# Five steps of the last slab moved from the seventh turn into the last one

## The chip, the cores and the metric

The kernel runs on one core of a Trainium2 chip. A core has a matrix engine (TensorE, PE in the profile; PEld are its weight loads), VectorE (DVE), ScalarE (ACT), GpSimd (POOL) and SyncE (SP), which here only issues DMAs. Each engine works through its own queue in order, and the queues wait for each other by semaphores. The metric is the device time of one execution in microseconds (us).

## The reference

2048 tokens (4 sequences of 512) are looked up in a table of 256 channels. An RWKV-7 attention layer follows (4 heads of 64 channels, a recurrence over the 512 positions), then a mixture of 8 experts, of which each token takes the likeliest.

```python
h = take(table, x) + bias
# attention on u = layernorm(h); xr, xw, xk, xv, xa, xg are mixes of u with its predecessor
r, k, v = xr @ Wr, xk @ Wk, xv @ Wv
a = sigmoid(a0 + xa @ a1 @ a2);  g = sigmoid(xg @ g1) @ g2
# ... kk, the decay w, and k changed by a; then for each position
S = S * wd + (S @ (-kk)) (kk * a)^T + v k^T;  y = S @ r
y = groupnorm(y) * ln_w + ln_b
y = y + (r * k * r_k).sum(per head) * v          # the bonus
h = h + (y * g) @ Wo
# experts
n = layernorm(h);  logits = (n @ w_red) @ normed(wg).T
e = argmax(softmax(logits));  score = max(softmax(logits))
h = h + score * (gelu(n @ W1[e] + b1[e]) @ W2[e] + b2[e])
```

## The kernel before

**Tiling.** The 512 positions are cut into 16 tiles of 32 positions by 4 sequences, 128 rows each, and two tiles make a slab; there are SLABS = 8 slabs. One call `build` emits the whole program, and every engine has a function `emit(step, i)` that holds what this engine does in a named step of slab i. All engines walk one list of (step, slab), made by `turns()` from two lists that are written out by hand: ORDER, with a step and by how many slabs it runs ahead of the turn (`P.lg:1` is done in turn 6 for slab 7), and LAST, the order of the last turn and of the expert tiles. Nothing is planned at run time.

**Steps.** F and P steps make a slab's inputs to the recurrence. P.lv (line 1019) makes the low-rank projection of v, and in the same PSUM bank the logits' share of the slab's own rows and, for a slab three back (BEHIND), the share of its attention output zT. P.lg (1063) is g's first product and ScalarE's sigmoid (460), after which ScalarE goes back to its table with ln and exp. P.rt (1082) sums r*k*r_k per head, ScalarE copies the sums to el_T (482). R.e (1030) turns el_T to token order; VectorE reads from it rt, emb_lg and the logits of the slab three back (751). P.kP, P.ar, P.bP scale keys and queries by the decay, P.tokk and P.tokb (1087, 1093) turn them to token order, P.M makes the products within a slab, P.masks masks them. P.g (1068) is g's second product; ScalarE copies the gate (464), GpSimd multiplies it with ln_w to gw (329). P.q is GpSimd's alone: v times rt, plus ln_b, times the gate, qg (336). Q steps are the recurrence of a slab: X0, T0 to X3, T3 an inverse by halves, W, A, S the state and the output y for its two tiles. O steps are the group norm of y, gw and qg, the turn to zT (O.zT), the product with Wo (O.out) and the addition to the rows (O.add). Z.l (1040) makes logits from zT directly, for slabs from ALONE on; Z.c takes the largest. N steps are the second norm.

**What sets the order around the change.** PSUM banks are shared by name: bank 0 by P.lv, R.e, P.lg, P.tokk and P.g, bank 1 by P.rt and P.tokb, bank 7 by O.zT, Z.l, O.out and the state. P.tokk waits for el_kept and rt_ok, by which VectorE has read R.e (1089). Q.A0's second half waits for logits_ok when a slab lies behind ALONE (1203). In the last turn G and H steps count and list the rows of each expert (G for slabs 0 to 6, H for slab 7), SP writes the rows and then the norm's scalars to `kept` (275), GpSimd fetches rows by the lists from there (T.f, line 379) and writes results (T.s, 371). SP waits for qg_ok before the first scalars, GpSimd before the first fetch, and VectorE before G.list. The T steps are the 23 expert tiles: T.n norms, T.x turns (1378), T.h is the first product (1391) and gelu, T.o the second (1404).

The list that repeats in every turn, unchanged by the diff:

```python
ORDER = """Q.X0:0 F.xn:2 P.norm:1 O.red:-1 Q.T0:0 E.norm:2 P.v:1 Q.X1:0 P.lv:1 Q.T1:0 P.lwa:1 F.xT:2 E.turn:2 O.yn:-1 N.st:-2
Q.X2:0 P.vga:1 F.xx:2 Q.T2:0 E.fold:2 P.key:1 P.wup:1 Q.W0:0 O.zT:-1 P.lg:1 N.rs:-2 Q.X3:0 P.cum:1 P.vc:1 N.lm:-2 P.decay:1
P.rt:1 Q.T3:0 R.e:1 Z.l:-1 Q.A0:0 P.kP:1 P.ar:1 P.tokk:1 P.bP:1 Q.S0:0 P.k:2 P.M:1 F.stats:3 F.rstd:3 E.out:1 P.q:1 O.out:-1
Q.W1:0 P.g:1 Z.c:-2 O.add:-1 Q.A1:0 P.tokb:1 P.masks:1 Q.S1:0 O.sq:0 P.r:2""".split()
```

Of the kernel before, what the change touches and what calls it, by code (L numbers as in the profile page):

```python
# [19 lines left out]
NT = BLK * L  # L20
# [11 lines left out]
ALONE = SLABS - BEHIND  # L32
# [53 lines left out]
def build(nc, table, tokens, tok_bias, consts, W, w1, w2, a1, a2, v1, v2, g1, g2, wo_t, w_red, wg, W1, W2, b2, kept, out):  # L86
    ctx = ExitStack()
    with ctx:
# [213 lines left out]
        def _(pool):  # L302
# [11 lines left out]
            def emit(step, i):  # L314
# [75 lines left out]
        def _(act):  # L390
# [12 lines left out]
            def emit(step, i):  # L403
# [33 lines left out]
                elif step == "P.lv":  # L437
# [3 lines left out]
                    rows = slice(64, 64 + L + E if i >= BEHIND else 64 + E)  # L441
# [18 lines left out]
                elif step == "P.lg":  # L460
                    act.wait_ge(s["lg_ps"], n)
# [1022 lines left out]
```

## Time and profile before

| | us |
|---|---|
| median of 3 runs | 482.14 |
| the runs | 479.24, 482.14, 486.59 |
| the profiled execution | 479.76 |
| its span in the profile | 477.6 |

The span runs from the first to the last instruction; 2.2 us lie around it. In the profile a line L1046 is line 1046 of the kernel, and a step is known by its line. PEclk is the TensorE clock that was granted, as a share of 2.4 GHz: 0.50 is 1.2 GHz. An fp32 product counts as two matmuls. Matmuls overlap, so the us of neighbouring rows add up to more than the time between their starts.

### The profile page before, as it was taken

The page shows a single profiled execution, that of the slowest core. Times are in us where ns is not written, and L with a number is a line of the kernel's source. Part 1 is how long each engine was busy: PE and PEld are TensorE (multiplying, and loading weights), DVE is VectorE, ACT ScalarE, POOL GpSimd, SP SyncE. Part 2 cuts the span into 40 slices and gives each one's busy share as a digit, 9 for nine tenths or more (in the row PEclk, how much of TensorE's full clock was granted, in tenths as well). Part 3 has the DMA queues.
Part 4 walks back from the last instruction along what each step waited for, and adds up shares of the span by engine and source line. Part 5 has one row for each costly group of instructions (what it writes and reads, how often), then busy time and mean ns, then how long its engine had stood idle before and what let it go on. Part 6 is the DMA issues. An engine that isn't in the chain of part 4 may idle for free.

```text
span 477.6 us, 23442 instructions
## 1 busy us (share of the span) xinstructions
PE 419.4 (88%) x10651; PEld 337.1 (71%) x10651; DVE 307.3 (64%) x784; ACT 200.2 (42%) x418; POOL 168.6 (35%) x153
## 2 busy tenths in 40 slices
PE   0467999999999998999999999897896898999991
PEld 0345777777867876877777776786785797889981
DVE  3646878578478678859768857736387654545541
ACT  1276484484385376367347526411111341222220
POOL 4754422342433425215315313403002336545231
PEclk9996899999999999999999999876586899999996
DMA  8960000000000000000000000000004557656310
GB/s 275 323 268 1 3 5 4 4 4 5 27 4 5 27 3 5 25 5 4 4 27 4 5 26 5 3 26 5 4 16 137 219 190 254 208 188 195 111 44 23
DMA packets 14014, 32.15 MB, mean 67 GB/s; under 512 B 4121, under 2 KB 7068, under 8 KB 13788
## 3 DMA queue, kind: packets, MB, share of 16 engines
q1 hardware_dynamic: 10908, 22.47, 14.1%
q0 software_dynamic: 3008, 8.19, 5.2%
q8 instruction: 84, 1.38, 1.2%
q14 instruction: 14, 0.11, 0.1%
HBM read 25.50 MB, written 5.15 MB: 64 GB/s over the span
## 4 chain that ended last, share of the span: by engine, by line
PE 63%; issue 11%; DVE 7%; POOL 6%; ACT 6%; DMA 5%; POOLq 0%; DVEq 0%; ACTq 0%; SPq 0%
PE ps L970 7%; PE ps L977 6%; POOL out L371 4%; PE ps L982 4%; PE ps L1107 3%; PE ps L1391 3%; DMA arena<-kept,arena 2%; PE ps L989 2%; POOL arena L379 2%; PE ps L1249 2%; PE ps L1175 2%; PE ps L1058 2%; PE ps L1404 2%; PE ps L1081 2%; PE ps L1066 1%
## 5 line engine op out<-in xcount | busy, mean ns | idle before, releaser
L595 DVE SCALAR_TENSOR_TENSOR arena<-arena 128x256 f32<-128x256 f32 x96 | 47.8, 546 | 5.1 <-PE ps L1028 2.9
L1404 PE MATMUL ps<-arena 128*128 x184 | 44.4, 383 | 2.3 <-issue 1.3
L1391 PE MATMUL ps<-arena 128*128 128x128 f32 x368 | 46.3, 281 | 0.0
L1391 PEld LDWEIGHTS ps<-arena 128*128 128x128 f32 x368 | 45.6, 198 | 0.8
L371 POOL DMA_INDIRECT out<-arena x23 | 22.7, 985 | 51.2 <-DVE arena L929 50.6
L551 ACT ACTIVATE arena<-arena 128x512 f32<-128x512 f32 x23 | 14.5, 629 | 61.6 <-DVE arena L917 61.6
L1404 PEld LDWEIGHTS ps<-arena 128*128 128x128 f32 x184 | 33.1, 190 | 7.8 <-issue 4.0
L379 POOL DMA_INDIRECT arena<-kept,arena x23 | 22.5, 979 | 43.0 <-DMA kept<-arena 35.5
L970 PE MATMUL ps<-arena 128*128 128x256 f32 x128 | 35.5, 427 | 0.7 <-DVE arena L595 0.7
L977 PE MATMUL ps<-arena 128*128 128x256 f32 x128 | 34.7, 417 | 0.0
L322 POOL TENSOR_TENSOR arena<-arena 128x512 f32<-128x512 f32 x8 | 8.4, 1046 | 64.7 <-ACT arena L436 64.7
L970 PEld LDWEIGHTS ps<-arena 128*128 128x128 f32 x128 | 26.0, 213 | 5.7 <-issue 0.8
L977 PEld LDWEIGHTS ps<-arena 128*128 128x128 f32 x128 | 25.0, 205 | 4.7 <-issue 0.6
L925 DVE TENSOR_TENSOR arena<-ps,arena 128x256 f32<-128x256 f32 x23 | 9.8, 424 | 27.2 <-PE ps L1404 26.1
L343 POOL TENSOR_TENSOR arena<-arena 128x512 f32<-128x512 f32 x8 | 10.1, 1268 | 47.9 <-ACT arena L466 47.9
L396 ACT ACT_TABLE_LOAD x20 | 25.7, 1283 | 1.0 <-PEq L1476 0.8
L917 DVE TENSOR_TENSOR arena<-ps,arena 128x512 f32<-128x512 f32 x23 | 15.9, 690 | 13.2 <-PE ps L1391 13.1
L1000 PE MATMUL ps<-arena 128*128 128x128 f32 x32 | 5.6, 303 | 19.9 <-ACT arena L413 16.9
L319 POOL TENSOR_TENSOR arena<-arena 128x512 f32<-128x512 f32 x8 | 10.2, 1275 | 32.5 <-DVE arena L606 32.4
L982 PE MATMUL ps<-arena 65*128 65x256 f32 (+1 forms) x64 | 18.9, 420 | 1.0 <-issue 1.0
L1000 PEld LDWEIGHTS ps<-arena 128*128 128x128 f32 x32 | 3.6, 150 | 22.6 <-issue 22.6
L307 POOL DMA_INDIRECT arena<-table,arena x16 | 16.3, 1020 | 9.0 <-DMA arena<-tokens 4.4
(315 smaller groups left out, 1046.3 us busy)
## 6 DMA issues: line engine op xcount, KB each, us to landing
arena<-W SPq DMA_DIRECT2D x23, 514.0 KB, 5.0
arena<-W SPq DMA_DIRECT2D x8, 512.0 KB, 8.3
kept<-arena SPq DMA_DIRECT2D x8, 256.0 KB, 2.4
arena<-W SPq DMA_DIRECT2D x4, 256.0 KB, 4.8
arena<-b SPq DMA_DIRECT2D x1, 1024.0 KB, 15.9
arena<-consts SPq DMA_DIRECT2D x1, 849.0 KB, 4.8
arena<-kept,arena POOLq DMA_INDIRECT x23, 4.8
out<-arena POOLq DMA_INDIRECT x23, 2.5
```

Of the source, the lines that this page charges most:

```text
L307: pool.indirect_dma_start(out=res[:, t, :], out_offset=None, in_=table[:, :], in_offset=bass.IndirectOffsetOnAxis(ap=ids[:, t:t + 1], axis ...
L371: pool.indirect_dma_start(out=out[:, :], out_offset=bass.IndirectOffsetOnAxis(ap=(rows_u if i < FIRST else out_u)[:, i:i + 1], axis=0), in ...
L379: pool.indirect_dma_start(out=x_s[q % XB], out_offset=None, in_=kept[0:1 + 128 * (T1 if q < FIRST else TILES), :], in_offset=bass.Indirect ...
L396: A.preload_act_table_set(name)
L551: A.activation(hT[i % 2], h_pre[i % 2], ACT.Gelu).then_inc(s["act_ok"], 1)
L595: last = V.scalar_tensor_tensor(out=mix[j % 3][:, p, :], in0=xx[:, p].rearrange("p b t -> p (b t)"), scalar=mixed_by[MIXES[j]][:, p:p + 1] ...
L917: V.tensor_tensor(h_pre[b], ps[:, 2 + b, :].rearrange("p (m t) -> p m t", m=HC), W1_s[i % WB][:, 2 * HID:2 * HID + HC].unsqueeze(2).broadc ...
L970: last = mul(pair(ps[:, bank, :], h2), w[:, kt, h2 * 128:(h2 + 1) * 128], src[:, kt, :], start=kt == 0, stop=kt == 1)
L977: last = mul(ps[:, bank, c * C:(c + 1) * C], src[:, kt, c * 128:(c + 1) * 128], w[:, kt, :], start=kt == 0, stop=kt == 1)
L982: last = mul(ps[:, bank, c * C:(c + 1) * C], src[0:rows, c * 128:(c + 1) * 128], w[0:rows, :], start=True, stop=True)
L1391: last = mul(ps[:, 2 + b, m * 128:(m + 1) * 128], W1_s[i % WB][:, p * HID + m * 128:p * HID + (m + 1) * 128], x_sT[b][:, p, :], start=p == ...
L1404: last = mul(ps[:, 1, b * C:(b + 1) * C], hT[b][:, m, :], W2_sb[:, bass.ds(e * (HC * C) + m * C, C)], start=m == 0, stop=m == HC - 1)
```

## The change

ALONE goes from 5 to 4, so that slab 4's logits are made by a Z.l step of their own in turn 5, and P.lv and R.e of the last slab no longer carry them. P.rt, R.e, P.lg, P.g and P.q of slab 7 (HELD) leave turn 6 and stand in LAST, where Q.X0:7, Q.T0:7, Q.X1:7, Q.T1:7 and later steps are around them. LAST is a new list also beyond that: N.st:5 and N.rs:5, G and H steps and the expert tiles stand in another order. The waits follow: for slab 7, P.rt waits until bank 1 was read (tokb_ok), R.e until bank 0 was (tokk_ok), P.lg until VectorE has read R.e, P.g until the sigmoid is done; P.tokk waits for lv_ok in place of R.e's readers. In the last turn ScalarE loads the sigmoid's table before P.lg and the one of ln and exp behind it. The diff, cut to its changed lines, the lists to their beginnings:

```diff
 BEHIND = 3
-ALONE = SLABS - BEHIND
+ALONE = SLABS - BEHIND - 1
 T2 = TILES - T1
...
-LAST = """Q.X0:7 O.red:6 Q.T0:7 O.yn:6 Q.X1:7 Z.c:5 Q.T1:7 O.zT:6 Q.X2:7 N.st:5 N.rs:5 Z.l:6 Z.c:6 Q.T2:7 Q.W0:7 N.lm:5 Q.X3:7 G.cnt:0 Q.T3:7 Q.A0:7
-G.rank:0 Q.S0:7 Q.W1:7 Q.A1:7 Q.S1:7 O.out:6 O.sq:7 G.list:0 O.add:6 N.st:6 N.rs:6 O.red:7 N.lm:6 G.dif:0 G.exp:0 O.yn:7 G.score:0 G.own:0
-G.turn:0 O.zT:7 Z.l:7 G.rows:0 T.f:0 Z.c:7 H.cnt:0 H.rank:0 O.out:7 T.n:0 T.x:0 H.list:0 T.n:1 T.x:1 H.own:0 T.h:0 T.n:2 T.n:3 T.h:1 T.x:2
-O.add:7 N.st:7 T.o:0 N.rs:7 N.lm:7 H.dif:0 T.s:0 T.n:4 H.exp:0 H.score:0 T.x:3 T.n:5 T.h:2 T.o:1 T.x:4 T.s:1 H.turn:0 T.h:3 T.o:2 T.h:4 T.s:2
-H.rows:0 T.n:6 T.f:1 T.x:5 T.o:3 T.n:7 T.x:6 T.h:5 T.o:4 T.n:8 T.x:7 T.h:6 T.x:8 T.n:9 T.s:3 T.o:5 T.h:7 T.n:10 T.s:4 T.o:6 T.x:9 T.n:11 T.s:5
...
+LAST = """Q.X0:7 P.rt:7 O.red:6 Q.T0:7 R.e:7 O.yn:6 Q.X1:7 Z.c:5 P.lg:7 Q.T1:7 N.st:5 P.g:7 O.zT:6 Q.X2:7 Z.l:6 Z.c:6 Q.T2:7 N.rs:5 Q.W0:7 Q.X3:7 N.lm:5
+G.cnt:0 Q.T3:7 Q.A0:7 G.rank:0 Q.S0:7 Q.W1:7 Q.A1:7 Q.S1:7 O.out:6 G.list:0 O.add:6 O.sq:7 N.st:6 N.rs:6 O.red:7 N.lm:6 G.dif:0 G.exp:0 P.q:7
+O.yn:7 G.score:0 O.zT:7 G.own:0 G.turn:0 Z.l:7 G.rows:0 Z.c:7 H.cnt:0 H.rank:0 O.out:7 T.f:0 T.n:0 T.x:0 H.list:0 T.n:1 T.x:1 T.n:2 T.n:3
+T.h:0 T.x:2 H.own:0 T.h:1 T.o:0 T.n:4 T.x:3 T.n:5 T.h:2 O.add:7 T.s:0 T.o:1 T.s:1 T.x:4 N.st:7 N.rs:7 H.turn:0 T.n:6 N.lm:7 H.dif:0 H.exp:0
+H.score:0 T.h:3 T.x:5 T.o:2 T.s:2 H.rows:0 T.h:4 T.o:3 T.x:6 T.h:5 T.f:1 T.o:4 T.n:7 T.h:6 T.x:7 T.n:8 T.n:9 T.s:3 T.o:5 T.x:8 T.s:4 T.h:7
+T.x:9 T.s:5 T.o:6 T.n:10 T.s:6 T.n:11 T.h:8 T.x:10 T.n:12 T.o:7 T.h:9 T.x:11 T.o:8 T.h:10 T.x:12 T.s:7 T.n:13 T.n:14 T.o:9 T.h:11 T.s:8 T.s:9
...
+HELD = ["P.rt", "R.e", "P.lg", "P.g", "P.q"]
...
         for step, ahead in steps:
-            if 0 <= turn + ahead < SLABS:
+            if 0 <= turn + ahead < SLABS - (step in HELD):
                 yield step, turn + ahead
...
                 elif step == "P.g":
+                    if i == SLABS - 1:
+                        pool.wait_ge(s["g_ok"], n)
                     last = P.tensor_tensor(gw[par], gate, ln_w.unsqueeze(1).broadcast_to([128, CH, C]), ALU.mult)
...
                     after(act, "el_ps", i)
-                    rows = slice(64, 64 + L + E if i >= BEHIND else 64 + E)
+                    rows = slice(64, 64 + L + E if BEHIND <= i < SLABS - 1 else 64 + E)
                     A.copy(el_T[rows, :], ps[rows, 0, 0:NT]).then_inc(s["lv_ok"], 1)
...
                 elif step == "P.lg":
+                    if i == SLABS - 1:
+                        use("sigmoid_and_others")
                     act.wait_ge(s["lg_ps"], n)
-                    A.activation(low_g, ps[:, 0, 0:NT], ACT.Sigmoid)
+                    last = A.activation(low_g, ps[:, 0, 0:NT], ACT.Sigmoid)
+                    if i == SLABS - 1:
+                        last.then_inc(s["la_ok"], 1)
                     use("natural_log_exp_and_others")
...
                                     sd1[:, tiles].unsqueeze(2).broadcast_to([128, CH, E]), ALU.mult).then_inc(s["el_kept"], 1)
-                    if i >= BEHIND:
+                    if BEHIND <= i < SLABS - 1:
                         past = slice((i - BEHIND) * CH, (i - BEHIND + 1) * CH)
...
                     pe.wait_ge(s["fold_ok"], 2)
-                    if i >= BEHIND:
+                    if BEHIND <= i < SLABS - 1:
                         pe.wait_ge(s["fold_ok"], 3)
                         last = mul(ps[64:64 + L, 0, 0:NT], wl[:, kt, :], xT[:, kt, 1:CH + 1, :].rearrange("p c t -> p (c t)"), start=kt == 0, stop=kt == 1)
-                        if i >= BEHIND:
+                        if BEHIND <= i < SLABS - 1:
                             last = mul(ps[96:96 + E, 0, 0:NT], wol[:, kt, :], zT[:, kt, :], start=kt == 0, stop=kt == 1)
                     pe.wait_ge(s["invp_ok"], n)
+                    if i == SLABS - 1:
+                        pe.wait_ge(s["tokk_ok"], n)
                     after(pe, "el_kept", i)
                     for c in range(CH):
-                        m = 96 + E if i >= BEHIND else 64 + E
+                        m = 96 + E if BEHIND <= i < SLABS - 1 else 64 + E
                         last = nc.tensor.transpose(ps[:, 0, c * 128:c * 128 + m], el_T[0:m, c * 128:(c + 1) * 128], ident[0:m, 0:m])
...
                     after(pe, "xT_ok", i + 2, 1 * SLABS)
+                    if i == SLABS - 1:
+                        pe.wait_ge(s["el_kept"], n)
+                        pe.wait_ge(s["rt_ok"], n)
                     for kt in range(2):
                     pe.wait_ge(s["tokk_ok"], n)
+                    if i == SLABS - 1:
+                        pe.wait_ge(s["la_ok"], n + 1)
                     up_by_token(g2_sb, low_g, 0, 128).then_inc(s["g_ps"], 1)
...
                     pe.wait_ge(s["rk_ok"], n)
+                    if i == SLABS - 1:
+                        pe.wait_ge(s["tokb_ok"], n)
                     for h2 in range(2):
                     pe.wait_ge(s["kP_ok"], n)
-                    pe.wait_ge(s["el_kept"], n)
-                    pe.wait_ge(s["rt_ok"], n)
-                    after(pe, "logits_ok", i - BEHIND + 1)
+                    if i < SLABS - 1:
+                        pe.wait_ge(s["el_kept"], n)
+                        pe.wait_ge(s["rt_ok"], n)
+                        after(pe, "logits_ok", i - BEHIND + 1)
+                    else:
+                        pe.wait_ge(s["lv_ok"], n)
                     to_tokens(kP, 0).then_inc(s["tokk_ps"], 1)
```

## Rows read from the trace of the kernel before

**Rows 1.** Windows by turn: stretch, its length, each engine's busy us, PEclk, DMA, GB/s

```profile
246.60:284.40 37.80, 37.23 (x1261) 28.34 (x1264) 28.39 (x67) 21.15 (x43) 12.64 (x10) 1.00 0.04 12
284.40:324.00 39.60, 37.48 (x1251) 29.12 (x1254) 23.53 (x55) 16.60 (x34) 12.18 (x10) 0.87 0.03 10
324.00:372.90 48.90, 37.62 (x1050) 32.29 (x1038) 31.14 (x128) 6.33 (x18) 7.29 (x7) 0.65 0.20 62
```

**Rows 2.** Timeline of turn 5, TensorE: start, us, line, out<-in, count

```profile
266.35 0.67 PE L1200 MATMUL ps<-arena 32*32 32x64 f32 x32
...
269.76 1.99 PE L970 MATMUL ps<-arena 128*128 128x256 f32 x8
...
275.93 1.11 PE L1249 MATMUL ps<-arena 32*32 32x64 f32 x64
```

**Rows 3.** Timeline of turn 6, TensorE; in brackets idle before and its releaser

```profile
299.25 1.03 PE L1066 MATMUL ps<-arena 128*128 128x256 f32 x4
...
302.39 0.63 PE L1085 MATMUL ps<-arena 128*32 128x256 f32 x4
302.95 0.75 PE L1167 MATMUL ps<-arena 32*32 32x32 f32 x64
303.99 0.37 PE L1038 MATMUL ps<-arena 104*128 104x104 f32 x2 [0.28 <-ACT arena L485]
304.87 1.03 PE L1046 MATMUL ps<-arena 128*128 128x8 f32 x8 [0.51 <-DVE arena L761]
305.83 0.66 PE L1200 MATMUL ps<-arena 32*32 32x64 f32 x32
...
317.56 1.11 PE L1249 MATMUL ps<-arena 32*32 32x64 f32 x64
...
319.71 1.13 PE L982 MATMUL ps<-arena 128*128 128x256 f32 x4
```

**Rows 4.** Windows of turn 6 and the last turn, columns as in the first

```profile
307.00:316.00 9.00, 8.58 (x220) 7.20 (x217) 3.89 (x15) 0.58 (x1) 0.00 (x0) 0.50 0.01 4
...
324.00:327.00 3.00, 1.67 (x140) 1.33 (x128) 2.15 (x4) 1.11 (x3) 0.00 (x0) 1.00 0.02 5
327.00:331.00 4.00, 2.25 (x128) 1.98 (x128) 3.26 (x11) 0.00 (x0) 2.35 (x2) 0.50 0.03 6
331.00:345.00 14.00, 12.29 (x415) 10.94 (x419) 5.65 (x25) 1.46 (x4) 0.17 (x1) 0.50 0.02 5
```

**Rows 5.** Timeline, VectorE and ScalarE, in turn 6 and the last turn

```profile
300.70 1.28 ACT L396 ACT_TABLE_LOAD   x1
301.02 0.41 DVE L705 TENSOR_TENSOR arena<-ps,arena 128x256 f32<-128x256 f32 x1
302.00 0.30 ACT L517 ACTIVATE arena<-arena 128x2 f32<-128x2 f32 x1
...
332.38 0.58 ACT L554 COPY arena<-ps 128x512 f32<-128x512 f32 x1 [5.62 <-PE ps L1323]
```

**Rows 6.** Timeline of the last turn, TensorE

```profile
325.65 0.74 PE L1124 MATMUL ps<-arena 32*32 32x32 f32 x63 [0.93 <-DVE arena L678]
...
327.97 1.08 PE L1131 MATMUL ps<-arena 32*32 32x32 f32 x64 [1.00 <-DVE arena L684]
...
331.23 1.11 PE L1323 MATMUL ps<-arena 128*128 128x128 f32 x4 [0.47 <-POOL arena L350]
332.28 1.08 PE L1145 MATMUL ps<-arena 32*32 32x32 f32 x64
...
344.66 1.08 PE L1200 MATMUL ps<-arena 32*32 32x64 f32 x32 [0.52 <-DVE arena L709]
```

**Rows 7.** Timeline of the last turn, VectorE

```profile
349.25 0.34 DVE L951 TENSOR_SCALAR arena<-arena 128x128 f32<-128x128 f32 x1
...
356.12 0.69 DVE L736 TENSOR_TENSOR arena<-ps,arena 128x512 f32<-128x512 f32 x1 [0.45 <-PE ps L977]
```

**Rows 8.** Timeline of the expert tiles, TensorE

```profile
399.35 0.44 PE L1378 MATMUL ps<-arena 128*128 128x128 f32 x2 [1.82 <-DVE arena L913]
```

More of the change, by code:

```diff
@@ L57 @@
-O.add:7 N.st:7 T.o:0 N.rs:7 N.lm:7 H.dif:0 T.s:0 T.n:4 H.exp:0 H.score:0 T.x:3 T.n:5 T.h:2 T.o:1 T.x:4 T.s:1 H.turn:0 T.h:3 T.o:2 T.h:4 T.s:2
-H.rows:0 T.n:6 T.f:1 T.x:5 T.o:3 T.n:7 T.x:6 T.h:5 T.o:4 T.n:8 T.x:7 T.h:6 T.x:8 T.n:9 T.s:3 T.o:5 T.h:7 T.n:10 T.s:4 T.o:6 T.x:9 T.n:11 T.s:5
-T.h:8 T.x:10 T.o:7 T.h:9 T.x:11 T.s:6 T.o:8 T.n:12 T.s:7 T.h:10 T.x:12 T.o:9 T.n:13 T.h:11 T.x:13 T.s:8 T.o:10 T.s:9 T.s:10 T.n:14 T.n:15
-T.h:12 T.x:14 T.n:16 T.o:11 T.h:13 T.o:12 T.x:15 T.h:14 T.s:11 T.s:12 T.n:17 T.x:16 T.n:18 T.o:13 T.h:15 T.x:17 T.n:19 T.o:14 T.s:13 T.h:16
@@ L61 @@
-T.x:18 T.n:20 T.o:15 T.h:17 T.x:19 T.s:14 T.o:16 T.h:18 T.n:21 T.s:15 T.x:20 T.n:22 T.o:17 T.h:19 T.s:16 T.x:21 T.o:18 T.h:20 T.s:18 T.x:22
-T.s:17 T.o:19 T.s:19 T.h:21 T.o:20 T.s:20 T.h:22 T.o:21 T.s:21 T.o:22 T.s:22""".split()
+LAST = """Q.X0:7 P.rt:7 O.red:6 Q.T0:7 R.e:7 O.yn:6 Q.X1:7 Z.c:5 P.lg:7 Q.T1:7 N.st:5 P.g:7 O.zT:6 Q.X2:7 Z.l:6 Z.c:6 Q.T2:7 N.rs:5 Q.W0:7 Q.X3:7 N.lm:5
+G.cnt:0 Q.T3:7 Q.A0:7 G.rank:0 Q.S0:7 Q.W1:7 Q.A1:7 Q.S1:7 O.out:6 G.list:0 O.add:6 O.sq:7 N.st:6 N.rs:6 O.red:7 N.lm:6 G.dif:0 G.exp:0 P.q:7
@@ L63 @@
+T.x:13 T.o:10 T.s:10 T.h:12 T.x:14 T.o:11 T.n:15 T.h:13 T.x:15 T.n:16 T.n:17 T.s:11 T.o:12 T.h:14 T.x:16 T.o:13 T.h:15 T.s:12 T.o:14 T.s:13
+T.x:17 T.h:16 T.n:18 T.o:15 T.x:18 T.s:14 T.n:19 T.s:15 T.h:17 T.n:20 T.x:19 T.n:21 T.o:16 T.h:18 T.x:20 T.n:22 T.o:17 T.h:19 T.x:21 T.s:16
+T.o:18 T.s:18 T.h:20 T.x:22 T.s:17 T.o:19 T.h:21 T.s:19 T.o:20 T.h:22 T.s:20 T.o:21 T.s:21 T.o:22 T.s:22""".split()
+HELD = ["P.rt", "R.e", "P.lg", "P.g", "P.q"]
 MIXES = ["x_k", "x_r", "x_v", "x_w", "x_a", "x_g"]
```

## The prediction

> **What bounds the kernel now.** I read the stretches by turn first, then the order of time on TensorE in the turns of slabs 5, 6 and 7, then what the other engines did beside it. Turn 5 (in which slab 5 is in its Q steps and slab 6 in its P steps) takes 37.8 us, with TensorE busy 37.23 of them at a granted clock of 1.00; turn 6 takes 39.6 at 0.87; the last turn up to the first expert tile takes 48.9, TensorE busy 37.62, at 0.65 [rows 1]. So the full turns are bound by TensorE's queue, and the last turn by a chain between TensorE, VectorE and GpSimd that runs at half clock. What follows it, the 23 expert tiles, hardly depends on the change.
>
> Two places matter. In turn 6 the bonus turn R.e:7 starts at 303.99, 0.28 after its input; Z.l:5 waits for VectorE's logits behind it (idle 0.51) and runs 1.03; only then does Q.A0:6 start, at 305.83 [rows 3]. Right after this thin stretch the clock is 0.50 from 307 to 316 [rows 4]. In the last turn TensorE waits 0.93 before T0, 1.00 before X1 and 0.47 before the turn of z, each time for another engine [rows 6]; it is busy 1.67 of the 3 us after 324, and then the clock is 0.50 for the 14 us after 331 [rows 4]. These waits are the room into which the change puts its work.
>
> **Turn 5: one step more.** ALONE goes from 5 to 4, so slab 4's logits no longer ride in P.lv:7, they are a Z.l:4 of their own in turn 5, right behind R.e:6: eight weight loads and products of 8 columns, 1.03 on TensorE [rows 3], and one VectorE addition. TensorE waits there until logits_ok is 4, which VectorE gives in R.e:6; behind it in the queue stands all of Q.A0:5, and VectorE's P.kP:6, which P.tokk:6 wants, now stands behind the new addition. Turn 6 of before has exactly this pair: from R.e's end (303.99 and 0.37) to Q.A0 (305.83) 1.5 us, where turn 5 goes on at once. So +1.5 at least. The upper end is that the clock falls there too. From Q.A0 to Q.W1 turn 6 takes 305.83 to 317.56, 11.7 us [rows 3]; turn 5 takes 266.35 to 275.93, 9.6, of which 1.9 is P.k, that turn 6 has not [rows 2]: 7.7 at high clock, so a fall costs 4.0, and the sum is +5.5. P.k's dense products stand in turn 5 and should bring the clock back sooner than in turn 6. I take +3.5. P.lv:7 loses four products that run beside others on other columns: nothing, at most their own 0.4.
>
> **Turn 6: five steps less.** P.lg:7 (1.03), P.rt:7 (0.63), R.e:7 with its wait, and P.g:7 (1.13) leave TensorE [rows 3]; ScalarE loses an activation and two copies, VectorE the two reads of R.e, GpSimd the bonus products beside P.kP. Without P.lg and P.rt Q.T3:6 could start 1.5 earlier than 302.95; VectorE's mask before it ends at 301.43 and hangs on VectorE's own steps ahead of it, so it does not move [rows 5], so T3 starts about 301.5. Z.l:5 then follows T3 without a wait (logits_ok is long 5), 302.25 to 303.25, and covers VectorE's addition for Q.A0: A0 at about 303.3 in place of 305.83, 2.5 earlier. If the clock then stays high, A0 to W1 takes 7.7 and not 11.7: W1 at 311.0 for 317.56. P.g:7 stood between W1 and Q.A1 (319.71) [rows 3]; of its 1.06 some 0.3 turn into a wait for ScalarE's copy of w, 0.75 is won. Sum −7.3. If the clock falls as before, −2.5 and −0.75: −3.3. I take −7.3, as the idle of 0.28, 0.51 and the thin R.e ahead of the fall are gone. P.tokk:7 now waits only for kP and lv_ok, both earlier.
>
> **The last turn: five steps more, in the gaps.** P.rt (0.63) stands in T0's wait of 0.93, R.e (0.37) in X1's of 1.00, P.lg and P.g (1.03, 1.13) between X1 and the turn of z, whose wait is GpSimd's and ends at 331.2 anyway. ScalarE takes two more table loads (1.28 each [rows 5]) with an activation and two copies of at most 0.6 each, some 4 us, in an idle stretch of 5.62 before its copy of zT at 332.38 [rows 5]: nothing, as long as P.lg is done in time; with the cover gone it would be those 4. GpSimd takes P.g and P.q behind O.yn:6, where it has nothing until the first fetch, and TensorE's and SP's waits for qg_ok come much later: nothing, though VectorE's steps beside it stretch. VectorE's N.st:5 now stands before X2's mask, beside X2's products. The output's path is X2, T2, W0, X3, T3, A0, S0, W1, A1, S1, O.out:6, O.add:6, then the scalars, SP's write and the fetch: no step is new on it.
>
> High end: the filled gaps keep the clock up. X2 to A0 takes 332.28 to 344.66, 12.4 us at half clock [rows 6]; with turn 6's ratio (7.7 to 11.7) 8.1, 4.3 less. From A0's start to VectorE's first instruction of G.list at 349.25 it is 4.6, at that ratio 3.0, 1.6 less; from there on to O.add:6 at 356.12, which waited only 0.45 for TensorE [rows 7], G.list's 28 instructions on VectorE set the pace at any clock. Together −5.9. Low end: the clock falls as before and P.lg and P.g run at half speed in front of X2: T1 and the turn of z come 2.3 later (1.03 and 1.13 at the ratio 11.7 to 7.7 make 3.3, less some 1.0 for the waits that they fill, among them the 0.47): +2.3. TensorE would still idle some 2 us before X2, against 3.4, and the fall in turn 6 came behind less idle than that; but the dense products that now stand there should lift the clock before W0. I take −2.5.
>
> **The expert tiles.** Tile 7's turn starts at 399.35 after 1.82 idle for the late fetch; the new order has T.h:6 in front of T.x:7, and H.rows one T.h earlier: up to −1.8. Against it O.add:7 stands one tile later on VectorE, and behind it SP's second write of scalars, with the loads of W1 for tiles 6 and on behind that in SP's queue; the same wait again would be +1.8 [rows 8]. I take −1.0.
>
> **Sum.** 479.76 + 3.5 − 7.3 − 2.5 − 1.0 = 472.5 for an execution like the profiled one, whose span is 477.6 with 2.2 around it. The median of the runs shown is 2.4 above it and the runs spread by 7; I add 0.5 and say 473.0.
>
> **A page against a row.** In the rows ScalarE's table load takes 1.28 and the next activation begins 0.02 behind it (300.70, then 302.00) [rows 5]. The Trainium skill, "ScalarE: Activation LUTs", section "What ACT_TABLE_LOAD costs", adds a drain of about 1.38 to each switch, some 2.66 in all, and its table advises to group activations by set, which speaks against this change: P.lg's sigmoid alone in the last turn asks for two switches. By the page the copy of zT would come about 1.4 later and the sum be 473.9 in place of 472.5; by the row, which I follow, it is hidden.
>
> **Rivals.**
> 1. The clock holds through the last turn and does not fall in turn 5: 1.5 − 7.3 − 5.9 − 1.8 = −13.5, 466.3. For it: turn 5 and most of the run stand at 1.00 with small waits in them. Against: X0 to T1 is still a ping-pong with VectorE.
> 2. A wash: turn 5 falls fully (+5.5), turn 6 gains 7.3, last turn and tiles give nothing: −1.8, 478.0. For it: Z.l:4 copies the pattern ahead of turn 6's fall.
> 3. Slower, by the clock alone: the fall in turn 5 lasts as long as that of the last turn, which is low from 327 to 345 and on, 18 us at least [rows 4]. At 4.0 for the 9 us of turn 6 that costs 8.0, with Z.l's 1.5; then −7.3, the dense steps of the last turn at the low clock +2.3, and tiles −1.0: +3.5, 483.3. It decides from a low stretch of about 10 us (4.5 us of cost) in turn 5 on, provided that the last turn stays low. Against it: P.k and P.M follow at once in turn 5.
> 4. The change does not shorten turn 6: its path is VectorE's (P.key beside GpSimd, decay, P.kP), so only the low end, −3.3, comes: 479.76 + 1.5 − 3.3 = 478.0, as rival 2.
>
> **Chances.** My forecast with its own range of 468 to 477: 0.47; rival 1: 0.18; rivals 2 and 4 together: 0.25; rival 3: 0.10. The range 465 to 482 holds all but rival 3 and a rest of the others. A measurement of this kernel tells about 2% from no change, 472.5 and 491.8 against the median of 482.14: faster is rival 1 and half of the forecast, 0.40; slower 0.05, that part of rival 3 in which the low stretches are longer still; the rest, 0.55, is within 2%.
>
> **What would show it.** Right: in turn 6 Q.A0 starts directly behind Z.l, which starts directly behind T3; the granted clock is about 1.00 from there to X0:7, and turn 6 is near 32 us long; turn 5 is longer than 37.8, by 1.5 to 5.5; in the last turn TensorE has no idle over 0.5 between X0 and T1 but for VectorE's masks, and needs less time than before from X2 to O.add:6. Wrong: a low clock in turn 6 as before, X2 pushed back by P.g at half speed, the copy of zT waiting on ScalarE's table load, or tile 7 waiting longer than 1.82.

## The result and the profile after

The changed kernel takes 479.97 us (median of 20 runs), the kernel before 483.19 (20 runs): ratio 0.9932, 95% interval [0.9905, 0.9959], so 0.7% or some 3 us faster, where 1.9% was forecast. Executions of one kernel spread by up to 3%, and this ratio leaves out the slower ones, so it hangs on the fastest run. The profiled execution took 476.59, its span is 474.8 (before 479.76 and 477.6).

Windows by turn of the changed kernel, columns as in [rows 1] (turn 5, turn 6, the last turn to the first expert tile):

```profile
249.60:289.30 39.70, 38.27 (x1269) 29.34 (x1270) 27.64 (x68) 21.17 (x43) 12.49 (x10) 1.00 0.04 11
289.30:325.80 36.50, 32.97 (x1231) 25.69 (x1234) 22.02 (x52) 15.43 (x31) 7.71 (x6) 0.95 0.04 11
325.80:374.80 49.00, 38.63 (x1066) 31.73 (x1058) 32.23 (x134) 10.33 (x24) 12.75 (x12) 0.74 0.21 71
```

Turn 5 grew by 1.9, turn 6 shrank by 3.1 (forecast 7.3), and the last turn is as long as before although its clock is higher. The part of the program ahead of turn 5, which the change leaves alone, happened to be 3.1 longer in this profile (turn 5 begins at 249.6, before at 246.5; 244.2 to 251.7 in all 17 profiles), so the stretches say more than the spans. The order of turn 6 came as forecast up to Q.W1; then TensorE stood still inside Q.A1. Timeline of TensorE, turn 6 of the changed kernel (start, us, line, out<-in, count, idle before and what ended it):

```profile
306.97 0.75 PE L1186 MATMUL ps<-arena 32*32 32x32 f32 x64
307.65 1.06 PE L1055 MATMUL ps<-arena 128*128 128x8 f32 x8
308.64 0.66 PE L1219 MATMUL ps<-arena 32*32 32x64 f32 x32
...
316.42 1.42 PE L1268 MATMUL ps<-arena 32*32 32x64 f32 x64
...
319.21 0.42 PE L1294 MATMUL ps<-arena 32*32 32x64 f32 x14 [0.27 <-ACT arena L507]
321.16 0.52 PE L1294 MATMUL ps<-arena 32*32 32x64 f32 x18 [1.52 <-issue]
```

T3, Z.l and A0 (L1186, L1055, L1219) follow each other without a wait, and A0 to W1 (L1268) takes 7.8 us where it took 11.7 [rows 3]. The pause of 1.52 is ended by "issue": no engine is waited for. Two more of this kind stand in the last turn, in W0 and T3 (L1207, L1186):

```profile
340.14 0.25 PE L1207 MATMUL ps<-arena 64*32 64x64 f32 x2 [1.32 <-issue]
...
344.21 0.58 PE L1186 MATMUL ps<-arena 32*32 32x32 f32 x25 [0.97 <-issue]
```

And the clock fell: behind the pause in A1, and again between the two of the last turn. Windows of the changed kernel, cut where the granted clock changes:

```profile
321.90:328.80 6.90, 6.90 (x229) 5.14 (x221) 2.40 (x4) 2.24 (x7) 0.00 (x0) 0.51 0.02 5
328.80:342.40 13.60, 10.78 (x478) 8.94 (x474) 8.12 (x34) 4.71 (x8) 7.02 (x6) 1.00 0.02 5
342.40:352.60 10.20, 8.71 (x306) 7.55 (x305) 6.15 (x25) 0.37 (x1) 0.00 (x0) 0.50 0.01 3
```

Beside [rows 4] this says: the low stretch of turn 6's middle is gone, a new one stands at its end, and in the last turn 13.6 us are back at 2.4 GHz, but with pauses in them.

**What "issue" is here.** The page of the changed kernel lists, among the DMA queues:

```profile
q8 instruction: 84, 1.38, 1.3%
```

84 transfers of 16 KB bring TensorE's instructions. The page counts 10655 matmuls and as many weight loads, 21310 records: 254 per transfer. Two kernels below show that the queue is TensorE's: with 1920 records fewer (w_after) and with 256 more (f_thin) its line reads

```profile
q8 instruction: 77, 1.26, 1.1%
```

```profile
q8 instruction: 85, 1.39, 1.2%
```

By the start times of these transfers in the trace no two come closer than 3.3 us, in this kernel or the one before (3.2 in all 17 traces). In turn 6 of the changed kernel one lands at 319.65, and the pause in A1 ends 1.5 us later; in the last turn one lands at 338.67 and the pause in W0 ends 1.5 later, one at 342.95 and the pause in T3 ends 1.3 later. In the 17 traces of this document 53 pauses ended by issue are longer than 0.8 us, and every one ends 1.2 to 1.6 us after such a landing. (A pause of 0.72 in Z.l:7, the same in all, does not, and is another matter.) An inverse step (X or T) is 64 small matmuls and 64 loads in the profile's count, 128 records in 0.75 us; two such steps use up a transfer in 1.5 us. P.lg is 4 matmuls and 4 loads, 8 records in 1.03 us. So taking wide products out of a stretch would push the thin ones together until the queue runs dry; the experiments test it. The trace of before already has two such pauses, in T0:7 and T3:7, which the prediction's list of waits leaves out:

```profile
326.76 0.21 PE L1124 MATMUL ps<-arena 32*32 32x32 f32 x1 [0.38 <-issue]
...
343.62 0.53 PE L1167 MATMUL ps<-arena 32*32 32x32 f32 x19 [0.85 <-issue]
```

### The profile page after: what moved, and what is told of

Read it like the earlier page. It is cut to its first block, busy times and chain, and to the rows that moved or that the text cites. A ratio compares the mean times of both kernels' runs of the same rounds, so it can differ in the third digit from the quotient of the medians.

```text
span 474.8 us, 23457 instructions
## 1 busy us (share of the span) xinstructions
PE 417.1 (88%) x10655; PEld 333.5 (70%) x10655; DVE 305.3 (64%) x784; ACT 202.8 (43%) x420; POOL 167.7 (35%) x153
## 3 DMA queue, kind: packets, MB, share of 16 engines
q8 instruction: 84, 1.38, 1.3%
## 4 chain that ended last, share of the span: by engine, by line
PE 64%; issue 12%; POOL 7%; DMA 6%; ACT 5%; DVE 5%; POOLq 0%; DVEq 0%; ACTq 0%; SPq 0%
PE ps L977 7%; PE ps L984 6%; POOL out L374 4%; PE ps L989 4%; PE ps L1126 3%; POOL arena L382 3%; PE ps L996 2%; PE ps L1268 2%; PE ps L1067 2%; PE ps L1194 2%; PE ps L1078 2%; PE ps L1095 2%; PE ps L1089 1%; DMA out<-arena 1%; PE ps L1171 1%
## 5 line engine op out<-in xcount | busy, mean ns | idle before, releaser
L924 DVE TENSOR_TENSOR arena<-ps,arena 128x512 f32<-128x512 f32 x23 | 15.9, 690 | 11.3 <-PE ps L1410 11.2
L722 DVE TENSOR_TENSOR arena<-ps,arena 128x512 f32<-128x512 f32 x7 | 4.8, 692 | 24.8 <-PE ps L1328 24.8
```

Source lines behind the costliest of these rows:

```text
L924: V.tensor_tensor(h_pre[b], ps[:, 2 + b, :].rearrange("p (m t) -> p m t", m=HC), W1_s[i % WB][:, 2 * HID:2 * HID + HC].unsqueeze(2).broadc ...
```

## The experiments

**Theories.** Supply: the missing gain of turn 6 and of the last turn went into TensorE's instruction refills and the falls of the clock behind those pauses. Clock alone: the pauses are incidental. Rival C: the new order of the expert tiles, or the two added table loads, lost it.

The stretches, each the difference of two starts in a trace (turns 5 and 6 from Q.X0 to the next Q.X0; the last turn up to G.list:0's products; from there to the end), and the times. The last column is the mean of all runs of a kernel less the mean of the runs of the kernel before beside them, ± one standard error. For e2_old_tiles, e3_lg_back, b_new_tiles and a_fill the ratio lies above 1 and this column below 0; by the ratio e3_lg_back is slower than before and the other three can't be told from it. The text goes by the column and by the stretches.

| kernel | turn 5 | turn 6 | last turn | rest | ratio [95%] | us against before |
|---|---|---|---|---|---|---|
| before | 37.80 | 39.61 | 31.90 | 121.7 | 1 | 0 |
| changed | 39.67 | 36.50 | 31.11 | 117.9 | 0.9932 [0.9905, 0.9959] | −2.7 ± 1.0 |
| e0_after_again | 42.20 | 35.35 | 32.19 | 119.6 | 0.9977 [0.9907, 1.0047] | −3.1 ± 1.2 |
| e1_alone | 42.16 | 37.03 | 34.77 | 122.1 | 1.0171 [1.0056, 1.0287] | +3.2 ± 1.4 |
| e2_old_tiles | 42.39 | 34.28 | 31.97 | 122.2 | 1.0046 [0.9985, 1.0107] | −1.0 ± 1.3 |
| e3_lg_back | 42.27 | 33.90 | 35.16 | 119.0 | 1.0093 [1.0033, 1.0154] | −1.3 ± 0.9 |
| b_new_tiles | 37.88 | 40.11 | 32.38 | 120.1 | 1.0052 [0.9994, 1.0110] | −2.3 ± 1.0 |
| z_mid | 38.59 | 36.71 | 32.78 | 118.3 | 0.9973 [0.9934, 1.0012] | −4.1 ± 0.9 |
| w_before | 38.49 | 38.78 | 25.21 | 121.5 | 0.9855 [0.9798, 0.9913] | −6.5 ± 1.4 |
| w_after | 42.56 | 32.16 | 26.99 | 119.6 | 0.9778 [0.9713, 0.9842] | −13.0 ± 1.1 |
| f_wide | 42.20 | 35.32 | 34.00 | 118.2 | 0.9935 [0.9889, 0.9980] | −3.5 ± 1.3 |
| f_thin | 42.73 | 43.87 | 34.90 | 119.0 | 1.0135 [1.0067, 1.0204] | +6.0 ± 1.2 |
| z_fill | 37.86 | 35.21 | 36.47 | 119.2 | 0.9857 [0.9806, 0.9909] | −7.9 ± 1.1 |
| z_pg | 37.59 | 39.13 | 35.16 | 119.7 | 0.9878 [0.9807, 0.9949] | −6.1 ± 1.5 |
| b_fill | 37.74 | 38.45 | 34.44 | 122.5 | 1.0001 [0.9936, 1.0066] | −2.3 ± 1.1 |
| a_fill | 40.07 | 34.77 | 33.72 | 119.5 | 1.0018 [0.9964, 1.0073] | −3.9 ± 0.8 |
| z_fill2 | 37.41 | 39.27 | 34.03 | 118.1 | 0.9909 [0.9867, 0.9950] | −7.0 ± 0.9 |

**The changed kernel once more.** No edit.

> The changed kernel once more, beside the next three on one chip. Both theories expect a ratio near 0.993 to the kernel before. Supply theory (TensorE's instruction refills of 256 records don't come closer than about 3.3 us): pauses ended by nothing but issue of more than 1 us inside or next to Q.A1:6 (0.0 to 0.1 us there before) and between Q.T1:7 and Q.A0:7, some 5 us in all from R.e:6 to G.list:0, again. Clock theory (the pauses are incidental): the pauses are elsewhere or gone, and the low clock still begins near the end of the seventh turn.

By all runs the gain is the same 3 us; the ratio leaves it open. The pauses ended by issue are there again, at the same places, though the one in A1 is shorter than the 1 us that was expected:

```profile
317.54 0.52 PE L1294 MATMUL ps<-arena 32*32 32x64 f32 x18 [0.72 <-issue]
...
336.92 0.25 PE L1207 MATMUL ps<-arena 64*32 64x64 f32 x2 [1.32 <-issue]
...
341.54 0.58 PE L1186 MATMUL ps<-arena 32*32 32x32 f32 x25 [1.52 <-issue]
```

With 0.91 in X3 and 0.22 in P.M they make 4.7 us from Q.X0:6 to G.list:0 (1.2 before: 0.85 in T3:7, 0.38 in T0:7). New is turn 5: 42.2 in place of 39.7. Its timeline here, with Z.l:4 (L1055) and P.tokk (L996):

```profile
264.31 1.03 PE L1055 MATMUL ps<-arena 128*128 128x8 f32 x8 [0.51 <-DVE arena L768]
...
267.03 0.66 PE L996 MATMUL ps<-arena 128*128 128x128 f32 x4 [0.72 <-DVE arena L662]
```

and the window of 6.8 us behind it, at half clock:

```profile
267.60:274.40 6.80, 6.80 (x98) 5.02 (x101) 3.66 (x15) 0.70 (x2) 0.00 (x0) 0.50 0.01 2
```

Of the nine profiles in which Z.l:4 stands there, seven have this fall (42.2 to 42.7 us), two have not (39.7, 40.1); of the eight others none has a fall in turn 5 (37.4 to 38.6).

**One part alone.** The kernel before with nothing but Z.l:4 moved:

```diff
-ALONE = SLABS - BEHIND
+ALONE = SLABS - BEHIND - 1
```

and P.lv and R.e of the last slab without those logits.

> One part alone: the kernel before with only the logits of the fifth slab (Z.l:4) moved out of the turn of the seventh slab into the sixth turn. Prediction's steps: +3.5 us in the sixth turn as forecast, or +1.9 as the changed kernel's profile shows, against some 0.9 us (eight 256-column products and the shorter R.e) less in the seventh. Supply theory: the kernel is 1 to 2 us slower than before (ratio 1.002 to 1.004), since nothing thin is left closer together. Theory that the move of Z.l:4 itself lost the missing gain: 3 us or more slower (ratio over 1.006).

It is slower: +3.2 ± 1.4 (6 runs). Turn 5 pays 4.4, turn 6 gains 2.6 (the fall at its middle is gone), and the last turn gives 2.9 back: pauses ended by issue of 1.18, 1.11 and 1.45 stand in P.g:7, T0:7 and T3:7, with the clock low behind the last two. So the second reading of the expectation is the nearer one: Z.l:4 alone, at this place, costs more than it brings.

**The tiles.** The changed kernel with the old order from T.f:0 on, and the kernel before with the new order from G.turn:0 on; only the list is edited.

> The changed kernel with the last order of the kernel before from the first fetch for the expert tiles on. The prediction gave the new order of the tiles 1.0 us of gain (bounds 1.8 either way). If the prediction's term holds, this kernel is about 1 us slower than the changed one (ratio to before near 0.995); if the new order itself ate the missing gain (rival C), it is 2 us or more faster (0.989 or less); supply theory says nothing of the tiles: equal to the changed kernel within 1 us.

> The kernel before with nothing but the new order of the expert tiles (from G.turn:0 on). The stretch from G.list:0 to the end took 121.7 us before, 117.9 and 119.6 in two profiles of the changed kernel, 122.2 with the old order put back. If the order of the tiles is what shortens it, this kernel is 2 to 3 us faster than the one before (0.994 to 0.996), and the stretch takes 118 to 120 us. Rival (the prediction's own account: the order is worth 1.0 us, the rest comes from the steps moved out of the seventh turn): 0.997 to 1.000 and 120.5 us or more.

The order of the tiles is what shortens the rest: 121.5 to 122.5 us in the five profiles with the old order, 117.9 to 120.1 in the twelve with the new one. Alone it brings −2.3 ± 1.0 by all runs, nearly the gain of the whole change, and without it 1.6 to 2.0 (± 1.5) us of the gain go. The ratio of b_new_tiles, 1.0052 [0.9994, 1.0110], fits neither reading of its expectation, and its stretch of 120.1 lies between the two; it is the rest of all 17 profiles, in which the two orders don't overlap, that shows the gain.

Groups of TensorE's instructions in the expert tiles, the turn T.x, in the changed kernel with the new and with the old order (busy, mean ns, idle before and its releaser):

```profile
L1397 PE MATMUL ps<-arena 128*128 128x128 f32 x44 | 8.8, 282 | 0.0
```

```profile
L1397 PE MATMUL ps<-arena 128*128 128x128 f32 x42 | 8.4, 282 | 2.0 <-DVE arena L920 2.0
```

The wait of tile 7 for the late fetch [rows 8] is gone with the new order and back with the old one. Rival C's half about the tiles falls with the wrong sign.

**The gate back in turn 6.** P.lg:7 and P.g:7 return to ORDER's places; ScalarE's two added table loads go with them.

```diff
-HELD = ["P.rt", "R.e", "P.lg", "P.g", "P.q"]
+HELD = ["P.rt", "R.e", "P.q"]
```

> The changed kernel with the gate products P.lg and P.g of the last slab back in the seventh turn (so that ScalarE's two more table loads are gone too); P.rt, R.e and P.q stay in the last turn. Prediction's way of counting TensorE's time: P.lg and P.g are about 1.7 us of wide products that go back into the seventh turn and out of the last one, where they stood in waits: 1 to 2 us slower than the changed kernel (ratio to before 0.995 to 0.998). Supply theory: the seventh turn gets 12 wide products that take time but hardly any records, so its pause at Q.A1:6 shrinks by about as much: equal to the changed kernel or up to 1 us faster (0.991 to 0.993). Rival C (the gate's table loads lost the gain in the last turn): 2 us or more faster (0.989 or less).

In time it is 1.8 ± 1.2 us behind the second measurement of the changed kernel, as TensorE's time alone had it; supply had expected it level or ahead. Inside it both happened: turn 6, which has 1.7 us more of products, is 1.5 to 2.6 shorter (33.9; pauses ended by issue 0.42 in place of 1.9 and 2.4), and the last turn is 3 to 4 us longer: there TensorE pauses 1.75 in T0:7 and 1.17 in T3:7, with the clock low behind both. The pauses moved with the wide products. So the table loads didn't lose the gain.

**Fewer records, about the same time.** In the last two slabs each Q.X and Q.T step becomes two wide products with zeros as weights, in both kernels; the inverse of these slabs is left out beyond its first level. Of the eight steps, Q.X0:

```diff
-                    for u in range(UN):
+                    if i >= SLABS - 2:
+                        mul(ps[:, 4, 0:UN * L], zero_row[:, 0:128], flat(u_m), start=True, stop=False)
+                        last = mul(ps[:, 4, 0:128], zero_row[:, 0:128], flat(u_m)[:, 0:128], start=False, stop=True)
+                    for u in range(0 if i >= SLABS - 2 else UN):
```

> The kernel before, where the eight steps Q.X and Q.T of each of the last two slabs are two wide products with zeros as weights instead of 64 small ones (about the same time on TensorE, 8 records of the instruction stream instead of 256; the inverse of these slabs is left at its first level). Supply theory: with 16 steps poorer in records the refills are no bound any more; pauses ended by issue are under 0.5 us in all from Q.X0:6 to G.list:0 (1.2 before). Seventh turn and last turn to G.list:0: about 70 us (71.5 before). Clock theory: nothing moves but the clock.

> The changed kernel with the same replacement of Q.X and Q.T of the last two slabs (the inverse of these slabs is left at its first level). Supply theory: the pauses ended by issue (4.7 and 5.0 us in two profiles of the changed kernel) fall under 1 us, and from Q.X0:6 to G.list:0 it is 6 us or more shorter than its counterpart made from the kernel before (3.9 and 4.0 with the small products). Rival (the pauses only take the place of clock that falls anyway, or of waits for VectorE): the difference stays at 3 to 5 us.

(A step's small products are 128 records by the count above, not the 256 of the expectation.) Pauses ended by issue from Q.X0:6 to G.list:0 fell to 0.2 us in the kernel before and to 1.4 in the changed one (under 0.5 and under 1 were expected). Turn 6 of the pair, first before, then changed:

```profile
285.80:324.60 38.80, 37.42 (x765) 29.25 (x764) 23.20 (x55) 16.53 (x34) 12.39 (x10) 0.87 0.03 9
```

```profile
291.30:323.50 32.20, 30.72 (x748) 24.34 (x746) 21.35 (x52) 15.30 (x31) 7.92 (x6) 1.00 0.03 11
```

It differs by 6.6 us, close to the 7.3 of the forecast; with the small products it was 3.1 and 4.3. Term by term it is 2.6 up to A0 (2.5 forecast), 3.5 from there to W1 (4.0) and 0.5 behind W1 (0.75). The last turn is at 1.00 in the kernel before with the wide ones, first stretch, and only 25.2 us long; the second stretch is the changed kernel's:

```profile
324.60:349.80 25.20, 19.81 (x512) 16.03 (x505) 20.03 (x77) 4.29 (x11) 2.53 (x2) 1.00 0.01 3
```

```profile
323.50:350.50 27.00, 23.65 (x526) 18.81 (x519) 20.71 (x79) 8.18 (x16) 7.02 (x6) 0.94 0.01 3
```

Up to Q.W1 the two are level (18.40 and 18.35 us after Q.X0): at a high clock the steps put into the last turn cost nothing there and save nothing. The 1.8 us that the changed kernel loses come behind it, with a pause of 0.43 in W1 and a fall of the clock at 346.8, in which the eight products of O.out take 3.47 in place of 2.00. From Q.X0:6 to G.list:0 the pair is 4.8 apart, under the 6 that supply asked for; the two kernels as wholes are 6.5 apart.

**More records, same time.** Ahead of Q.X2:6 in the changed kernel, once three wide products, once 64 small ones, which the profile and the expectation count as 128 (the edits at the head of the step):

```diff
+                    if i == SLABS - 2:
+                        for twice in range(3):
+                            mul(ps[:, 4, 0:256], cst["ident"], cst["tri"][:, 0:256], start=True, stop=True)
```

```diff
+                    if i == SLABS - 2:
+                        for twice in range(2):
+                            for u in range(UN):
+                                for b in range(B):
+                                    q = quarter(b)
+                                    mul(ps[q, 4, u * L:(u + 1) * L], cst["low"][q, 0:L], cst["eye"][q, :], start=True, stop=True)
```

> The changed kernel with three extra 256-column products (constants into bank 4, not used) ahead of Q.X2:6, where TensorE waited 0.88 us for VectorE in both profiles of the changed kernel. Both theories: hidden in that wait, within 0.5 us of the changed kernel; seventh turn 35.3 to 36.5 us.

> The same place with 128 extra 32x32 products (256 records of the instruction stream; as two X steps take, some 1.4 us on TensorE) instead of three wide ones. Counting TensorE's time alone: 1.4 us less 0.88 of wait, so the seventh turn 0.5 us longer than with the wide ones. Supply theory: one refill more, 3.3 us apart from the next, so the seventh turn is 2.5 to 3.5 us longer than with the wide ones, or the pauses ended by issue from there to G.list:0 grow by that.

An fp32 product of 256 columns counts as two matmuls and took 0.5 us, so the two fillings turned out equal on TensorE: 1.56 and 1.38 us. Timeline with the wide and with the small ones (the filling, then Q.X2:6):

```profile
297.83 1.56 PE L1162 MATMUL ps<-arena 128*128 128x256 f32 x6
299.32 0.75 PE L1167 MATMUL ps<-arena 32*32 32x32 f32 x64
```

```profile
299.56 1.38 PE L1165 MATMUL ps<-arena 32*32 32x32 f32 x126
...
300.79 0.68 PE L1170 MATMUL ps<-arena 32*32 32x32 f32 x59
303.96 0.31 PE L1170 MATMUL ps<-arena 32*32 32x32 f32 x3 [2.49 <-issue]
```

The wide ones cost nothing (f_wide −3.5 ± 1.3 against before, the changed kernel −2.7). The small ones cost 9.5 ± 1.3 us more than the wide ones, seven times their time on TensorE: a pause of 2.49, and from within it on 13.7 us at half clock:

```profile
303.10:316.80 13.70, 12.84 (x281) 10.04 (x282) 7.37 (x11) 5.75 (x11) 4.41 (x4) 0.50 0.01 4
```

This is the plainest witness for supply, and the price is well above the 2.5 to 3.5 it had named: the pause is 2.5 of it, and 13.7 us at half clock make some 4.7 more, an estimate by the ratio of 7.7 to 11.7 us from A0 to W1 in the prediction.

**Another place for Z.l:4.** Ahead of Q.T2:6, with waits for slab_ok, s_sum and logits_ok set anew:

```diff
-            if 0 <= turn + ahead < SLABS - (step in HELD):
+            if (step, turn) == ("Q.T2", SLABS - 2):
+                yield "Z.l", ALONE
+            if 0 <= turn + ahead < SLABS - (step in HELD) and (step, turn + ahead) != ("Z.l", ALONE):
```

> The changed kernel with the logits of the fifth slab (Z.l:4) moved out of the sixth turn into the seventh, ahead of Q.T2:6, where TensorE waited 0.41 us; four waits are set anew so that bank 7 and zT stay safe. In the sixth turn Z.l:4 delayed VectorE's kP and so P.tokk, and in four of five profiles the clock fell to half there (the turn took 42.2 to 42.4 us, against 37.8 before and 39.7 in the profile of the changed kernel). If that loss is due to the place of Z.l:4, the sixth turn is back at 37.5 to 38.5 us, the seventh grows by 0.3 to 1.0, and the kernel is 3 to 4 us faster than the changed one (ratio to before 0.984 to 0.987). Rival (the clock falls once in this region wherever the work stands): the fall moves a few us and the time stays (0.992 to 0.995).

Turn 5 is back at 38.6 and at clock 1.00; in VectorE's order kP no longer stands behind Z.l's addition, and P.tokk does not wait. But turn 6 stays long (36.7: the pause in A1 is 1.25 here, with a fall behind it), and the kernel is only 1.1 to 1.5 us ahead of the changed one by all runs, which is within the error. That lies between the two readings of the expectation, nearer to the rival.

**The gate's second product later.** On top of z_mid, `P.g:7` stands behind `Q.T2:7`.

> The kernel with Z.l:4 ahead of Q.T2:6, and P.g:7 (four 256-column products, 1.13 us) moved in the last turn from behind Q.T1:7 to behind Q.T2:7, ahead of Q.W0:7, where 1.3 to 1.5 us of pause ended by issue stands. Counting TensorE's time alone: Q.X2:7 1 us earlier, Q.A0:7 as late as before, equal time (0.990 to 0.993). Supply theory: the pause in Q.W0:7 shrinks by about 1 us and Q.A0:7 comes up to 1 us earlier; if the fall of the clock near 342 us then stays out, up to 3 us faster (0.985).

The result is −6.1 ± 1.5, by all runs 2 us better than z_mid, about one error. The pause in W0 is gone, 0.6 is left in T3 of 1.7; but 1.4 came up in T1:7, from where P.g was taken, so the reading of the stretches is not clean: this profile also has a fall at 292.8, behind the wait ahead of X2:6, that z_mid's lacks.

**Filling the pauses.** On top of z_mid, on the changed kernel and on the kernel before, 26 products of no use where TensorE stands still; z_fill2 adds 23 to z_pg:

```diff
+FILL = {("Q.A1", 6): 4, ("Q.X1", 7): 2, ("Q.W0", 7): 5, ("Q.T3", 7): 5, ("Q.A0", 7): 1, ("Q.S1", 7): 1, ("O.zT", 7): 8}
...
+                if FILL.get((step, i)):
+                    pe.wait_ge(s["rk_ok"], SLABS)
+                    for _ in range(FILL[step, i]):
+                        mul(ps[:, 1, 0:256], cst["ident"], cst["tri"][:, 0:256], start=True, stop=True)
```

> The kernel with Z.l:4 ahead of Q.T2:6, and 26 extra 256-column products (constants into bank 1, not used) in seven places where TensorE stood still: 4 ahead of Q.A1:6, 2 ahead of Q.X1:7, 5 ahead of Q.W0:7, 5 ahead of Q.T3:7, 1 each ahead of Q.A0:7 and Q.S1:7, 8 ahead of O.zT:7. They are some 6.5 us of work at 2.4 GHz with few records. Counting TensorE's time alone: the waits for other engines hide 3 to 4 us, the rest is lost, so equal to 3 us slower than the kernel without them (ratio to before 0.99 to 0.998). Supply and clock theory (records come in during the extra products, and the falls of the clock at 321, 342 and 362 us follow pauses that are no longer there): the pauses ended by issue shrink by 3 us or more, the clock is at 1.0 over most of the last turn, and the kernel is 3 us or more faster (0.985 or less).

> The kernel before with 26 extra 256-column products (constants into bank 1, not used) where TensorE stands still in the last two turns: 4 ahead of Q.A1:6, 2 ahead of Q.X1:7, 5 ahead of Q.W0:7, 5 ahead of Q.T3:7, 1 each ahead of Q.A0:7 and Q.S1:7, 8 ahead of O.zT:7; at 0.48 us each, as such a product took in the other kernel with them, 12.5 us of work at 2.4 GHz. Clock theory: the falls at 327 and 361 us shrink or go, and the kernel is 2 to 5 us faster than before in spite of the added work (0.990 to 0.996). Counting TensorE's time alone: some 6 us slower.

> The changed kernel with the same 26 extra products in the same seven places. If the moved steps are worth what was forecast once the clock holds in both kernels, this one is 6 us or more faster than the kernel before with the extra products; if they are worth little at either clock, the difference stays at the 3 us of the two kernels without them. Ratio to before: 0.983 to 0.988 by the first, 0.987 to 0.993 by the second.

> The kernel with Z.l:4 ahead of Q.T2:6 and P.g:7 behind Q.T2:7, with 23 extra products placed by the pauses that were left: 4 ahead of Q.A1:6, 4 ahead of Q.T0:7, 1 ahead of Q.X1:7, 2 ahead of Q.W0:7, 4 ahead of Q.T3:7, 1 ahead of Q.A0:7, 2 ahead of Q.W1:7, 1 ahead of Q.S1:7, 4 ahead of O.zT:7. If pauses ended by issue are what drops the clock, the falls behind Q.T0:7 (323.7 us) and Q.W1:7 (351.0 us) go and the kernel is 1 to 4 us faster than the one with 26 (0.976 to 0.983). If only the amount of the products counts, it is equal or slower (0.983 to 0.988).

The added work is 12.5 us of TensorE (26 at 0.48), twice what the first expectation says. It costs nothing in any kernel: b_fill is at −2.3 ± 1.1 by all runs, the lower end of what the clock theory expected, and at none by the ratio. z_fill has the lowest mean of the versions that leave nothing out, ahead of both kernels: ratio 0.9857 [0.9806, 0.9909], −7.9 ± 1.1, against −4.1 without the filling. The mean clock of its six runs is 0.967 to 0.980, of z_mid's twelve 0.927 to 0.951. Its pauses in A1:6 and W0:7 are gone; one of 1.89 in T0:7 stayed (with a fall at its end), and the last turn of the profiled execution is long; that execution, 477.1 us, is the slowest of the six. a_fill and b_fill, which also differ by the order of the tiles, are 1.7 ± 1.1 apart, the second reading of the expectation: also with a better clock the moved steps are not worth 6 us. The clock did not hold in all of either (0.80 in the last turn of b_fill, 0.95 in a_fill), so this pair bounds the answer rather than gives it. z_fill2 removed the pauses in T0 and W1 as meant and is no faster than z_fill, where 1 to 4 us were expected if such pauses drop the clock: placing the products by the remaining pauses was not worth more.

## Why the prediction was right or wrong

**Turn 5, +3.5.** Mechanism and bounds held: Z.l:4 waits 0.51, its addition on VectorE delays kP, P.tokk waits 0.58 to 0.72, and the clock may fall. Measured +1.9 and +2.3 without the fall and +4.4 to +4.9 with it (forecast +1.5 and +5.5). The middle value stood for an either-or; seven of nine profiles are near the upper end.

**Turn 6, −7.3: the failed step.** A0 directly behind Z.l, 7.8 from A0 to W1, W1 6.05 us earlier in the turn (27.16 after Q.X0 against 33.21 before; 6.55 forecast): all came. What failed is the term of P.g:7 between W1 and Q.A1, of which "0.75 is won", with the clock held up to Q.X0:7: there 2.9 was lost. From W1 to Q.X0:7 before took 6.40, after 9.34 (7.89 in the second profile). The pause of 1.52 in A1 and the half clock behind it, by which the way from there to Q.X0:7 takes 4.15 in place of 2.60, make most of it. The sum counted every wide product at its TensorE time and none at the time in which it lets the records of thin products come in. Where the small products of X and T were gone, turn 6 did shrink by 6.6, and by 0.5 behind W1.

**The last turn, −2.5.** Measured −0.8 to G.list:0, and +0.3 in the second profile. The gaps did take the moved steps (X2 comes 8.57 after Q.X0 against 8.32), X2 to A0 ran at 2.4 GHz for most of its way, and still took 10.97 against 12.38 and not 8.1, as 2.3 us of pauses ended by issue stand in W0 and T3, and the clock fell at 342.4. The clock had come back at 328.8, ahead of P.lg (330.56) and P.g, the dense products by which the prediction let it rise. The high end, −5.9, was priced from the ratio of two stretches in which only 0.25 of such pauses stood; the wide version of the kernel before shows that such a last turn exists (X2 to A0 in 7.82, 25.2 in all), but not with these records.

**The tiles, −1.0.** Under-sized: 3.0 between the means of the twelve and the five profiles. The step named, T.h:6 ahead of T.x:7 and H.rows earlier, took away the whole wait of 1.8; the counter-risk on W1's loads did not show. Of the 3.0, 2.4 lie between the first T.x and the last T.o and 0.6 ahead of them; what made the part beyond the wait was not followed.

**The sum.** +1.9 to +4.4, −3.1 to −4.3, −0.8 to +0.3, −3.0: −5.0 to −2.6 for −7.3 forecast; measured −3. The direction was right and the time lies within 465 to 482, but outside the forecast's own 468 to 477, and the gain is a third of the forecast. That there is a gain is luck in good part, as it came for the most part by another term than named: the moved steps came to about nothing (e2_old_tiles: −1.0 ± 1.3), the order of the tiles brought it. Rival 2, the wash, was nearer in turn 5 and in the last turn, no nearer in turn 6, and further off in the tiles. Rival 1 needed a clock that holds, and it didn't; of rival 3, the fall in turn 5 came, but for 6.8 us and not for 18.

**The page against the row.** ScalarE, last turn of the changed kernel:

```profile
332.13 1.28 ACT L399 ACT_TABLE_LOAD   x1
334.00 0.59 ACT L473 COPY arena<-ps 128x512 f32<-128x512 f32 x1 [0.59 <-PE ps L989]
334.49 0.59 ACT L561 COPY arena<-ps 128x512 f32<-128x512 f32 x1
```

The copy after the load waits for TensorE's P.g, and the copy of zT (L561) follows at once; e3 without the two loads won nothing. Hidden, as the row had it. Whether the drain that the Trainium skill, "ScalarE: Activation LUTs", section "What ACT_TABLE_LOAD costs", adds behind a load is there can't be told at these two loads, where the next instruction waits anyway.

**Open.** That a pause makes the clock fall is the order in which they come, not shown for each: the pair of waits in turn 5 was followed by a fall seven times in nine, and the wait of 0.88 ahead of X2:6 in z_pg and z_fill2 but not in the changed kernel, e0, e1 or z_mid. Whether a pause or the thin products around it decide, these runs do not part: the small products in f_thin brought both. A fall needs no pause ended by issue: w_before has one from 307.1 to 317.3, in turn 6, behind waits of 0.46 for ScalarE and 0.51 for VectorE.

## What to carry to other kernels

Before taking wide matrix products out of a stretch of small ones, count the records (products and weight loads) that remain per us, and look for waits ended by "issue" in the trace of before: where a few stand already (0.85 and 0.38 here), the stretch is near its supply limit, and the removed time can come back as pauses. Two places for the same step differ by the queue behind it on the other engine: Z.l:4 made turn 5 longer by 1.9 to 4.9 us where VectorE's next operand stood behind its addition; with Z.l:4 elsewhere turn 5 was 0.8 longer, though the whole kernel won only 1.1 to 1.5. And the part of a change that looks like a by-product (here the order of the tiles) deserves a run of its own.

## What the runs showed of the hardware

TensorE's instructions arrive in transfers of 16 KB for about 254 records, never under 3.2 us apart in these traces, and each of the 53 pauses of more than 0.8 us that no engine ended was over 1.2 to 1.6 us after such a landing. In one place 128 small matmuls more cost 9.5 us where as much time in wide products cost nothing. And 12.5 us of useless wide products, put where TensorE would stand still, made the kernel with Z.l:4 in its new place 3.8 us faster (−7.9 against −4.1), while the granted clock rose from about 0.94 to 0.97.
